# Expert weights loaded in parts behind the shifts of separate attention units, zeroing of routed rows moved to a later layer, new order of steps

## What is computed

```python
x = layernorm(x + mamba(x))                 # layer 0: scan over 256 steps
x = layernorm(x + attention(x, ctx))
x = layernorm(x + ffn(x))                   # attention, rms norms, then 8 experts of 256 with w1_0, w2_0
x = layernorm(x + self_attention_wide(x))   # layer 1
x = layernorm(x + attention(x, ctx))
x = layernorm(x + moe(x))                   # 8 experts of 256, w1_1, w2_1
x = layernorm(x + causal_attention(x))      # layer 2
x = layernorm(x + masked_attention(x, ctx)) # adj and mask added to the scores
x = layernorm(x + moe(x))                   # 8 gated experts of 512, w1_2, w3_2, w2_2; rows are routed
x = layernorm(x + linear_attention(x))      # layer 3
x = layernorm(x + attention(x, gathered ctx))
x = layernorm(x + moe(x))                   # 8 experts of 256, w1_3, w2_3
```

## Time and profile before

| | |
|---|---|
| median of three runs | 1355.61 us (1353.09 to 1360.19) |
| profiled execution | 1361.56 us, its span 1359.6 us |
| PE (TensorE matmul) busy | 1226.2 us, 90% |
| DVE, ACT, POOL busy | 907.1, 693.2, 328.2 us |
| DMA moved | 93.06 MB, mean 68 GB/s |
| DMA issues on SP of expert weights (line 866) | 6 x 1024 KB, 3 x 2048 KB |

### The profile page before, as it was taken

How to read it: one execution, slowest core, us unless ns; L and a number is a source line. 1 busy time by engine, 2 the same in 40 slices (tenths; PEclk the granted TensorE clock), 3 DMA queues, 4 the chain that set the end, 5 groups by cost and what they waited for, 6 DMA issues and landing times. The chain is left out here.

```text
span 1359.6 us, 25527 instructions
## 1 busy us (share of the span) xinstructions
PE 1226.2 (90%) x8636; PEld 742.5 (55%) x8645; DVE 907.1 (67%) x2363; ACT 693.2 (51%) x1528; POOL 328.2 (24%) x443
## 2 busy tenths in 40 slices
PE   6778798899989998998969999999988999998898
PEld 2235344557656664675524444565555667665566
DVE  7995667666667787646548674233868988965544
ACT  4443476664344446673445434534655465456453
POOL 4554022001111111011212312122154444411001
PEclk9988999899989999998979999999998999999999
DMA  7006223011332122021652210311010000131121
GB/s 215 1 12 212 85 72 95 25 64 58 90 125 65 48 97 69 33 71 40 189 205 65 74 49 9 109 45 51 7 46 1 1 1 16 55 115 56 56 68 43
DMA packets 75789, 93.06 MB, mean 68 GB/s; under 512 B 6536, under 2 KB 60272, under 8 KB 73840
## 3 DMA queue, kind: packets, MB, share of 16 engines
q1 hardware_dynamic: 74640, 89.34, 20.6%
q0 software_dynamic: 1024, 2.10, 0.5%
HBM read 64.25 MB, written 28.67 MB: 68 GB/s over the span
## 5 line engine op out<-in xcount | busy, mean ns | idle before, releaser
L1461 ACT ACTIVATE P<-bank 128x512 f32<-128x512 f32 (+1 forms) x448 | 226.4, 597 | 104.0 <-PE bank L1157 103.3
L1873 DVE TENSOR_REDUCE mx<-bank 128x2 f32<-128x512 f32 x320 | 195.3, 681 | 79.1 <-PE bank L1128 78.9
L1042 PE MATMUL bank<-identb 128*128 128x512 bf16 x619 | 173.3, 393 | 3.0 <-DVE res L1803 1.5
L1674 POOL TENSOR_SCALAR rstd<-mv 128x2 f32<-128x2 f32 x56 | 15.3, 273 | 527.6 <-DVE mv L1725 435.0
L1170 PE MATMUL bank<-P,V 128*32 128x256 f32 (+1 forms) x1536 | 98.3, 375 | 7.6 <-ACT P L1461 7.1
L2021 DVE TENSOR_TENSOR room<-room 128x512 f32<-128x512 f32 x96 | 62.2, 699 | 58.8 <-DMA room<-gate_rows 32.4
L1128 PE MATMUL bank<-QKR 48*128 48x256 bf16 (+1 forms) x896 | 81.4, 275 | 16.4 <-DMA QKR<-split_rows 6.4
L1042 PEld LDWEIGHTS bank<-identb 128*128 128x128 bf16 x619 | 50.5, 99 | 81.3 <-issue 42.0
L1268 PE MATMUL bank<-xT,room 128*128 128x256 f32 x384 | 93.4, 393 | 0.0
L1274 PE MATMUL bank<-room 128*128 128x256 f32 x384 | 91.8, 386 | 0.7 <-DVE room L2021 0.7
L1157 PE MATMUL bank<-QKR 50*128 50x256 bf16 (+1 forms) x896 | 80.1, 274 | 7.3 <-ACT P L1461 3.3
(11 more groups left out here) (288 smaller groups left out, 2437.9 us busy)
## 6 DMA issues: line engine op xcount, KB each, us to landing
QKR<-split_rows SPq DMA_DIRECT2D x112, 192.0 KB
room<-gate_rows SPq DMA_DIRECT2D x48, 256.0 KB, 3.8
split_rows<-parts SPq DMA_DIRECT2D x56, 192.0 KB, 2.3
split_rows<-parts SPq DMA_DIRECT2D x56, 128.0 KB, 2.0
room<-in_w SPq DMA_DIRECT2D x6, 1024.0 KB, 8.8
room<-in_w SPq DMA_DIRECT2D x3, 2048.0 KB, 18.3
split_rows<-parts SPq DMA_DIRECT2D x56, 64.0 KB, 1.7
room<-in_mask SPq DMA_DIRECT2D x4, 512.0 KB, 5.7
```

Of the source, the lines that this page charges most:

```text
L1042: nc.tensor.matmul(bk[:, :], identb[:, :], identb[:, :].unsqueeze(1).to_broadcast([128, 4, 128]), start=True, stop=True, skip_group_check= ...
L1461: nc.scalar.activation(P[:, (e - 1) % NBUF_P, 0:width], psum(st, p)[:, 0:width], ACT.Exp, scale=SCALE).then_inc(read[k], 1)
L1873: V_.reduce_max(to, sc[:, :].rearrange("p (t s) -> p t s", t=TPB), AX.X).then_inc(read[k], 1)
```

## The change

1. `("LD", "w", m)` for m = 1 and 2 is split. `("LD", "part", 1, 0)` loads w1_1 and may be listed after the second-half SHIFT of unit 9; `("LD", "w", 1)` loads w2_1 after that of unit 10. `("LD", "part", 2, 0)` loads w1_2 after the second-half SHIFT of unit 21, `("LD", "part", 2, 1)` loads w3_2 after that of unit 22, and `("LD", "w", 2)` loads w2_2 after that of unit 23. The semaphore waits for the memory to be free stand with the first part. The layer 3 load is as before.
2. `("LD", "zero")` may be listed only after the second-half SHIFT of unit 12.
3. The planner's tables: SP costs of RH 0.9 to 1.25, RL 1.8 to 2.5, ROWS 2.8 to 3.1, SHIFT 1.3 to 1.4, GL 0.35 to 0.47, LD 0.1 to 1.0; LD landing 14.0 to 2.5; a new term by which every DMA step also adds its kilobytes to one shared transfer clock at 400 KB/us, and is done no sooner than 2.0 us behind it. SM on VectorE 1.25 to 1.27, MO 0.86 to 0.87.
4. The limits on banks: family `up` (MH, DH, DG) 5 to 3, `out` (PV, ZV) 4 to 5.
5. `FAVOUR`: 36 values changed and 8 added (of 149), in all stages.

No instruction of the compute engines is added or removed but FILL matmuls, whose number and place follow from the new order. The list of steps comes out of the planner anew, so the order can differ everywhere.

```diff
-    "QK": ((PE, 0.86), (ACT, 1.7)), "RH": ((SP, 0.9),), "SPLIT": ((POOL, 0.75), (ACT, 0.75), (POOL, 2.0)), "RL": ((SP, 1.8),), "ROWS": ((SP, 2.8),),
+    "QK": ((PE, 0.86), (ACT, 1.7)), "RH": ((SP, 1.25),), "SPLIT": ((POOL, 0.75), (ACT, 0.75), (POOL, 2.0)), "RL": ((SP, 2.5),), "ROWS": ((SP, 3.1),),
...
+KB_PER_US = 400.0
+KB = {"RH": 256, "RL": 512, "ROWS": 768, "SHIFT": 8, "GB": 8, "GL": 256, "BL": 192, "YS": 192, "LW": 1024,
+      ("LD", "w"): 2048, ("LD", "part"): 2048, ("LD", "wide"): 1024, ("LD", "mask"): 1536, ("LD", "mask2"): 512, ("LD", "mask3"): 512, ("LD", "lin"): 2048,
+      ("LD", "select"): 576, ("LD", "ctx"): 128, ("LD", "zero"): 1920}
...
-    out += [[("LD", "zero")], [("LD", "w", 1), ("LD", "w", 2), ("LD", "lin"), ("LD", "select"), ("LD", "w", 3)], [("LD", "wide")], [("LD", "mask"), ("LD", "mask2"), ("LD", "mask3")],
+    out += [[("LD", "zero")], [("LD", "part", 1, 0), ("LD", "w", 1), ("LD", "part", 2, 0), ("LD", "part", 2, 1), ("LD", "w", 2), ("LD", "lin"), ("LD", "select"), ("LD", "w", 3)], [("LD", "wide")], [("LD", "mask"), ("LD", "mask2"), ("LD", "mask3")],
...
-            return [("MO", m - 1, B - 1, *expert_units(m - 1)[-1])] + ([("ZV", B - 1, NH - 1)] if m == 2 else [])
+            return [("LD", "part", m, m - 1), ("SHIFT", *((SELF_WIDE, 2) if m == 1 else (MASKED, B - 1)), 1)]
+        if r[0] == "part":
+            m, i = r[1:]
+            if i:
+                return [("LD", "part", m, i - 1), ("SHIFT", MASKED, 2, 1)]
+            return [("MO", m - 1, B - 1, *expert_units(m - 1)[-1]), ("SHIFT", *((SELF_WIDE, 1) if m == 1 else (MASKED, 1)), 1)] + ([("ZV", B - 1, NH - 1)] if m == 2 else [])
         if r[0] == "zero":
-            return [("LC", 1, 1, 1)]
+            return [("LC", 1, 1, 1), ("SHIFT", 3, 0, 1)]
...
-MOST = {"score": 4, "prob": 4, "up": 5, "mamba": 6, "out": 4, "feat": 2, "turn": 3, "mix": 4}
+MOST = {"score": 4, "prob": 4, "up": 3, "mamba": 6, "out": 5, "feat": 2, "turn": 3, "mix": 4}
...
+        if kbytes(st):
+            moved = max(moved, t - cost(st)[-1][1]) + kbytes(st) / KB_PER_US
+            done[st] = max(done[st], moved + 2.0)
...
+                        load(w1s[m], f"w1_{m}", experts_in)
+                    load(w2s[m], f"w2_{m}", experts_in)
+                elif st[:2] == ("LD", "part"):
+                    m = st[2]
+                    if st[3]:
+                        load(w3, "w3_2", experts_in)
                     else:
                         full(sp, ("MO", m - 1, B - 1, *last_unit(m - 1)))
-                    if m == DISPATCHED:
-                        full(sp, ("ZV", B - 1, NH - 1))
-                        sp.wait_ge(norm_done, max(count[("NORM", SUB_OF[("moe", 0)], b)] for b in range(B)))
-                    load(w1s[m], f"w1_{m}", experts_in)
-                    if m == 2:
-                        load(w3, "w3_2", experts_in)
-                    load(w2s[m], f"w2_{m}", experts_in)
+                        if m == DISPATCHED:
+                            full(sp, ("ZV", B - 1, NH - 1))
+                            sp.wait_ge(norm_done, max(count[("NORM", SUB_OF[("moe", 0)], b)] for b in range(B)))
+                        load(w1s[m], f"w1_{m}", experts_in)
```

More of the change, by code:

```diff
@@ L60 @@
     "GQ": ((PE, 0.43), (ACT, 0.3)), "GS": ((PE, 0.43), (DVE, 1.7)), "GT": ((PE, 0.44), (ACT, 0.5)), "GM": ((PE, 0.86), (ACT, 0.3)),
-    "QK": ((PE, 0.86), (ACT, 1.7)), "RH": ((SP, 0.9),), "SPLIT": ((POOL, 0.75), (ACT, 0.75), (POOL, 2.0)), "RL": ((SP, 1.8),), "ROWS": ((SP, 2.8),),
+    "QK": ((PE, 0.86), (ACT, 1.7)), "RH": ((SP, 1.25),), "SPLIT": ((POOL, 0.75), (ACT, 0.75), (POOL, 2.0)), "RL": ((SP, 2.5),), "ROWS": ((SP, 3.1),),
     "V": ((PE, 0.44), (DVE, 0.42)), "Z": ((PE, 0.86), (ACT, 0.48)),
-    "BIAS": ((DVE, 1.15),), "SM": ((PE, 0.24), (DVE, 1.25)), "MS": ((DVE, 0.36),), "MT": ((PE, 0.15), (ACT, 0.3)), "SHIFT": ((SP, 1.3),),
+    "BIAS": ((DVE, 1.15),), "SM": ((PE, 0.24), (DVE, 1.27)), "MS": ((DVE, 0.36),), "MT": ((PE, 0.15), (ACT, 0.3)), "SHIFT": ((SP, 1.4),),
     "P2": ((PE, 0.24), (ACT, 0.98)), "PV": ((PE, 1.0), (ACT, 0.33)), "ZV": ((PE, 0.95), (DVE, 0.8)),
     "OT": ((PE, 0.43), (DVE, 0.48)), "OX": ((PE, 0.22), (ACT, 0.33)), "Y": ((PE, 0.44),),
-    "GATE": ((PE, 0.3), (DVE, 2.6)), "RANK": ((PE, 0.45), (DVE, 0.6)), "GB": ((PE, 0.42), (ACT, 0.3), (SP, 0.35)), "GL": ((SP, 0.35),),
+    "GATE": ((PE, 0.3), (DVE, 2.6)), "RANK": ((PE, 0.45), (DVE, 0.6)), "GB": ((PE, 0.42), (ACT, 0.3), (SP, 0.35)), "GL": ((SP, 0.47),),
     "MH": ((PE, 0.86), (ACT, 0.6)), "HG": ((DVE, 0.64),), "XG": ((DVE, 0.36),), "MG": ((PE, 0.86), (DVE, 0.67)),
-    "BI": ((PE, 0.22),), "MO": ((PE, 0.86),), "YC": ((ACT, 0.33),), "YT": ((PE, 0.22),),
+    "BI": ((PE, 0.22),), "MO": ((PE, 0.87),), "YC": ((ACT, 0.33),), "YT": ((PE, 0.22),),
     "SLOT": ((PE, 0.6), (DVE, 2.2)), "EID": ((PE, 1.0),), "SC": ((POOL, 2.6),), "BL": ((SP, 0.5),), "BT": ((PE, 0.35), (ACT, 0.42)),
@@ L71 @@
     "BP": ((POOL, 5.4),),
-    "LC": ((PE, 1.1), (ACT, 0.35)), "LW": ((SP, 0.1),), "LD": ((SP, 0.1),),
+    "LC": ((PE, 1.1), (ACT, 0.35)), "LW": ((SP, 0.1),), "LD": ((SP, 1.0),),
     "LF": ((PE, 0.86), (DVE, 2.6), (ACT, 1.15)), "LS": ((DVE, 1.46), (POOL, 1.95)), "LK": ((DVE, 0.85),), "LT": ((PE, 0.44), (ACT, 0.48)),
@@ L76 @@
 }
-LANDING = {"SC": 2.2, "BL": 2.5, "YS": 2.2, "YG": 2.2, "RL": 2.1, "ROWS": 4.2, "SHIFT": 3.2, "GB": 2.2, "GL": 2.5, "LD": 14.0, "LW": 4.0}
+LANDING = {"SC": 2.2, "BL": 2.5, "YS": 2.2, "YG": 2.2, "RL": 2.1, "ROWS": 4.2, "SHIFT": 3.2, "GB": 2.2, "GL": 2.5, "LD": 2.5, "LW": 4.0}
+KB_PER_US = 400.0
+KB = {"RH": 256, "RL": 512, "ROWS": 768, "SHIFT": 8, "GB": 8, "GL": 256, "BL": 192, "YS": 192, "LW": 1024,
+      ("LD", "w"): 2048, ("LD", "part"): 2048, ("LD", "wide"): 1024, ("LD", "mask"): 1536, ("LD", "mask2"): 512, ("LD", "mask3"): 512, ("LD", "lin"): 2048,
+      ("LD", "select"): 576, ("LD", "ctx"): 128, ("LD", "zero"): 1920}
 HOP = 0.15
@@ L498, in favour, with kbytes @@
     return FAVOUR.get(st[0] + stage_of(st), FAVOUR.get(st[0], 0.8))
+def kbytes(st):
+    return KB.get(st[0], KB.get(st[:2], 0))
 def plan():
@@ L509, in plan @@
     in_table = [None]
+    moved = 0.0
     def bank_time(st, t):
```

25 lines of the change are left out of this document (13 added, 12 removed).

## The result

The changed kernel takes 1321.22 us (median of four runs, 1318.92 to 1322.74) against 1355.47 us for the kernel before (now four runs, 1353.09 to 1360.19). The ratio is 0.9742, 95% interval 0.9711 to 0.9773: 34 us faster, where 15.6 us was forecast. The profiled execution has a span of 1317.2 us.

The account below looks back on a forecast made before the run. No engine bounds the whole span; places where PE stands count. Profiled 1361.56 - 12 - 4 - 1 + 1 = 1345.6 us, and 6.0 us less for the median gives 1340 us; range 1320 to 1357.

Parts of the forecast that it names:

- What bounds the kernel: Whole span: no engine bounds it; places where PE stands count, with 306.7 us of idle time and FILL together.
- Layer 2 weights, -12: Unit 17's shift rows at 683: PE's 10.4 us wait goes, plus 1.6 us of half clock; bounds -5.2 and -14.
- shared bandwidth: Layer 2 load: if transfers were shared evenly, the wait has another cause, that term is near 0, the sum 1352.
- Zeroing, -4, and +1 for its new place: PE's 2.80 us wait at 138.10 goes, -4 (0 to 6); stores after 509.51 come late, +1 (0 to 2).
- Layer 1 weights, -1: PE's 3.60 us wait at 378.71: only 0.7 us is due to these loads; far bound 7.
- Other places of the loads, 0: Loads behind shifts of units 9, 10, 21 and the group ending at 835.0 delay nothing needed soon: 0 us.
- Bank limits and order, 0 with 17 us either way: All stages: new limits and order taken as 0; eleven sublayer borders at 1.58 us each give 17 us either way.
- a better order: Whole kernel: planner with nearer SP and DMA costs takes 14 us more out of the 306.7: 1326; chance 0.17.
- Given back later: After 683, half the 10.4 us returns at the second half's shift and zeroing brings nothing: 1349; 0.22 with loads misplaced.
- Slower by the bank limit: Expert matrices: three banks make PE wait for ACT or DVE: 1365; chance 0.13 with a worse order.
- the change doesn't do what it says: New order puts 2 MB loads before due shifts again, bringing back 7 to 13 us: 1352; part of the 0.22.
- What would show it: Signs: no `QKR<-msT` wait over 2 us, six stores under 5 us, clock near 1.00, FILL 150 to 190 us.

Follow-up runs that it names:

- layer 2 alone: Kernel before, its own order, only the three layer 2 weight loads moved behind the second shifts of units 21, 22 and 23: 0.9916 to the kernel before.
- layer 1 alone: Kernel before, its own order, only the layer 1 loads moved behind the second-half shifts of units 9 and 10: 0.9995 to the kernel before.
- loads alone: Kernel before, its own order, all weight loads and the zeroing moved: 0.9842, 0.9883 and 0.9885 to the kernel before, mean 0.987.
- the joined list: Kernel before with all loads moved, old order except the new order between the outputs of units 15 and 17: 0.9837 to the kernel before.

## Why the prediction was right in the loads and wrong in the order

- *What bounds the kernel: right.* The useful matmuls stayed the same. Of the 42.4 us between the profiles 30.3 came out of idle time, 2.3 out of FILL and 9.8 out of the busy time of useful matmuls, which the prediction had only as clock terms of 1.6 and 1.2 us.
- *Layer 2 weights, -12: right.* 11.4 us by the runs, 12.2 in the stretch, and both halves of the term had their size. The Trainium skill (DMA: Bandwidth & Descriptors, Queues, rings and completion order) says that each engine takes the descriptors of a queue in ring order. The trace of before agrees: the first shift, 4 KB sent at 678.31, released PE only at 693.52, and with the 6 MB gone from in front the shifts are on time. By the other reading, shared bandwidth, the prediction had put this term near 0. The runs alone do not tell the two apart, since with the 6 MB gone nothing large is in front either way; it is the row of before that does.
- *Zeroing, -4, and +1 for its new place: direction right, too small.* 6.1 us net (3.5 to 8.7 by the interval), for 3. The gain was the far bound of 6, and the new place cost nothing that can be seen. The clock of 120 to 140 was not the reason: it is 0.87 with the zeroing moved, and 0.73 in the changed kernel. PE's work comes earlier instead (111 matmuls in the window for 84). The clock of the 20 us behind may be part of it: 1.00 with the zeroing moved alone and 0.91 to 1.00 with all loads moved, but 0.95, 0.87 and 0.77 in the three profiles (before, layer 2 alone, layer 1 alone) that have the old order and the zeroing in its old place.
- *Layer 1 weights, -1: right.* 0.7 us, within the error of none. Reading that wait against an undisturbed trip of rows was what kept it from being counted.
- *Other places of the loads, 0: right.* The first part has 2048 KB ahead of four row loads at 761.74, and no wait of PE for rows over 3.1 us is in the list. The three loads of 2048 KB land 7.5 to 8.1 us after their issue, so the last is there by 805.67 + 8.1 = 814, and the first DH runs at 837.18. The +1 for the zeros in their new place is not seen in any run.
- *Bank limits and order, 0 with 17 us either way: the step that failed.* It was worth 14 us more. Full kernel, mean of four ratios 0.9763; loads alone, 0.9870; the difference is 0.0107 x 1355.6 = 14.5 us, and 13.8 to 16.4 in the one set that ran both. The rival *a better order* (1326, 14 us more) is what happened. I had taken 0 because no row shows an order, and because many changed favours can undo good places: two arguments set against each other, and neither had a number. The runs show that the three tables fit each other, and that the gain lies in two stretches. In the first, between units 15 and 17, PE was idle for 19.0 us before and filled for 15.6, and only 10.4 of those 34.5 were the loads' wait; I had read the 20 us windows for the one big wait and didn't price what is left. But that row alone would not have given the answer. The stretch up to unit 15 had idle time and FILL of 164.6 us and gained nothing by the order, and that from unit 23 to 24 had 57.3 and gained 9 us. The size of the bound was fair (the measured time lies 1 us inside the range of 1320 to 1357); the value within it was not chosen from anything.
- *Rivals.* Given back later: no, except in the joined list, where 7.3 of 13.2 us came back at once, by rows that were late and not by shifts. Slower by the bank limit: no. Waits of PE for ACT at the two expert matrices come to 0.8 us each, and putting the old limits back made the kernel 11 us slower, not faster. That the change doesn't do what it says: no.
- *What would show it.* Six stores in 3.71 us, clock 1.00 and 19.88 of 20 us busy in 660 to 680, no wait for the shift rows, zeros behind unit 12's second shift (505.25), unit 1's first scores (128.38) without a DMA wait, FILL 171 us: all as written.

## What to carry to other kernels

A large load on a queue costs what stands right behind it. For the largest one here the term came out to 1 us from three rows: the issue of the load, its landing, and the wait of the engine that arrives; the smaller one, the zeroing, was worth twice its term. A planner's tables are to be taken as one set: putting any one of the three back cost 11 to 36 us here, and the new favours alone gave nothing. When a change replaces them together, idle time and FILL bound what the order can give but don't say where or whether it does: the stretch with most of both gained nothing here. A 0 for such a term needs a reason as much as any other value, and the term stays the widest of the sum.

## What the runs showed that was not expected

In some executions ACT and DVE stand in the routed stage for a releaser that the trace doesn't know. In the profile of before:

```profile
DVE res L1803 <- remote: 11.8, 1, 11.8
ACT room L1569 <- remote: 5.5, 3, 2.3
```

In a later profile of the changed kernel both engines stand beside GpSimd's indirect DMAs; its first profile has no such waits:

```profile
890.20 0.69 DVE L2050 TENSOR_TENSOR room<-bank,room 128x512 f32<-128x512 f32 x1 [3.73 <-remote]
...
914.28 0.27 ACT L1553 COPY room<-bank 128x128 f32<-128x128 f32 x1 [4.86 <-remote]
```

The stage from unit 23 to unit 24 takes 353.6 and 352.7 us in the two profiles of the changed kernel without these stalls, 364.7 and 365.3 in the two with them. With the loads alone it takes 362.8 without, 377.6 and 372.9 with them. So some 10 to 15 us belong to the execution and not to the kernel, and they are in the profile of before: against 362.8 the changed order gains 9.2 us in this stage, not 19.6. In the experiments they came where the kernel before took 1365 to 1367 us and were missing where it took 1353 to 1355; the profiled execution of before, 6 us above its median, has them as well. Two sets on chip 1 differ in it, so it is not a matter of the chip alone. In the sets with these waits the changed kernel has 0.9785 and 0.9782, in those without them 0.9742 twice. There the loads alone have 0.988, so the order may be worth 19 us rather than 14, but no such set ran both. What holds the two engines was not settled; nothing was run on it.
